# At a group's border, TensorE projects behind the contraction instead of in front of it, and VectorE takes first and adds later

## The reference, cut to what matters

```
x = x + conv(group_norm(x))      # 8 groups, 9 taps each, sampled bilinearly at learned places
    out = dcn_sample(v, deform, weights)      # v = x @ v_w + v_b
    return out.reshape(b, h, w, G * C) @ out_w + out_b
t = t + attention(layer_norm(t)) # 8 heads, 32 slices each: softmax(logits / temp), eidetic, out
t = t + experts(layer_norm(t))   # top 2 of 8 experts, 128 -> 512 -> gelu -> 128
```

## Time and profile before

| | us |
|---|---|
| median of 3 runs | 1312.51 |
| lowest and highest | 1308.49, 1313.44 |
| the profiled execution, its own time | 1311.18 |
| its span in the trace | 1309.4 |

### The profile page before, as it was taken

The page is one execution under the profiler, slowest core; times in us unless marked ns, Lnnn a source line. Parts: engine busy times, 40 slices in busy tenths (PEclk is TensorE's granted clock), DMA queues, the critical chain, the costliest instruction groups (busy, mean ns, idle before and its releaser), DMA issues.

```text
span 1309.4 us, 50781 instructions
## 1 busy us (share of the span) xinstructions
PE 992.3 (76%) x22310; PEld 807.6 (62%) x22310; DVE 829.8 (63%) x1651; ACT 773.7 (59%) x1431; POOL 688.0 (53%) x652
## 2 busy tenths in 40 slices
PE   4577785868788766998778758997887767787784
PEld 3455564656556655887466546886465656556684
DVE  5766757685766855557658746557578657446254
ACT  2676665777577572667767554667577545245352
POOL 2564545565645485444855693436755766003274
PEclk9689797998799787999988878999898878798997
DMA  6702130132100222364110322652110320444513
GB/s 161 158 24 53 54 68 23 68 56 68 28 26 19 58 80 76 113 176 119 48 48 24 97 72 70 172 167 63 48 41 25 108 82 3 133 132 142 162 43 95
DMA packets 142733, 104.80 MB, mean 80 GB/s; under 512 B 43649, under 2 KB 125890, under 8 KB 142002
## 3 DMA queue, kind: packets, MB, share of 16 engines
q1 hardware_dynamic: 138194, 92.68, 26.1%
q0 software_dynamic: 4320, 8.86, 2.3%
HBM read 76.32 MB, written 25.19 MB: 78 GB/s over the span
## 4 chain that ended last, share of the span: by engine, by line
PE 50%; ACT 17%; DVE 16%; issue 8%; POOL 7%; DMA 2%; SPq 0%; DVEq 0%; POOLq 0%; ACTq 0%
PE ps L1011 13%; PE ps L995 10%; PE ps L1226 6%; ACT xsb L1374 6%; PE ps L1019 5%; PE ps L1238 4%; DVE asb L1715 4%; ACT asb L1392 2%; POOL ysb L868 2%; PE ps L951 2%; POOL picked L834 2%; DVE ysb L1706 2%; DVE region L1942 2%; DVE x_tok L1985 2%; ACT region L1464 2%
## 5 line engine op out<-in xcount | busy, mean ns | idle before, releaser
L868 POOL TENSOR_TENSOR ysb<-ysb,rw 128x576 f32<-128x576 f32 x300 | 336.5, 1143 | 345.5 <-DVE ysb L1706 345.3
L995 PE MATMUL ps<-xsb,ysb 64*64 64x96 f32 x11008 | 328.6, 270 | 121.4 <-DVE asb L1715 30.1
L995 PEld LDWEIGHTS ps<-xsb,ysb 64*64 64x64 f32 x11008 | 278.3, 149 | 181.9 <-issue 89.0
L1374 ACT ACTIVATE xsb<-xsb,pick 128x576 f32<-128x576 f32 (+1 forms) x480 | 336.7, 751 | 5.2
L1715 DVE COPY asb<-ps 128x960 f32<-128x960 f32 (+1 forms) x208 | 215.9, 1044 | 115.9 <-PE ps L1011 106.0
L857 POOL TENSOR_TENSOR ysb<-rw,count 128x576 f32<-128x576 f32 (+1 forms) x150 | 174.8, 1165 | 70.6 <-PE ps L995 70.0
L1011 PE MATMUL ps<-asb,vd 32*32 32x258 f32 x8192 | 185.0, 391 | 24.4 <-issue 13.0
L1383 ACT ACTIVATE osp<-ps 128x258 f32<-128x258 f32 x128 | 43.0, 444 | 249.2 <-PE ps L1011 249.2
L1011 PEld LDWEIGHTS ps<-asb,vd 32*32 32x32 f32 x8192 | 124.6, 103 | 74.2 <-issue 42.4
L1464 ACT ACTIVATE region<-ps,b_col 128x128 f32<-128x128 f32 x368 | 104.9, 369 | 103.3 <-PE ps L1226 103.1
L1692 DVE TENSOR_TENSOR xsb<-rw,ps 128x576 f32<-128x576 f32 (+1 forms) x150 | 108.0, 720 | 54.7 <-PE ps L995 53.8
(11 more groups left out here) (304 smaller groups left out, 1203.3 us busy)
## 6 DMA issues: line engine op xcount, KB each, us to landing
ring<-in_L_ffn_W SPq DMA_DIRECT2D x122, 256.0 KB, 3.4
vd<-group_values SPq DMA_DIRECT2D x128, 128.0 KB, 2.7
set_rows<-ring SPq DMA_DIRECT2D x4, 1376.0 KB, 6.6
rw<-set_rows SPq DMA_DIRECT2D x30, 172.0 KB, 3.3
group_values<-region SPq DMA_DIRECT2D x32, 128.0 KB, 3.5
asb<-in_L_ffn_W SPq DMA_DIRECT2D x16, 256.0 KB, 5.1
region<-sorted_rows SPq DMA_DIRECT2D x6, 512.0 KB, 5.2
expert_rows<-region SPq DMA_DIRECT2D x6, 512.0 KB, 5.0
```

The costliest lines, as they stand in the source:

```text
L868: pl.tensor_tensor(ysb[:, ch % DEPTH, 0:sets, u, :], ysb[:, ch % DEPTH, 0:sets, NU - 1, :], rows_of(ig)[:, 2 + u, first:first + sets].rear ...
L995: last = pe.matmul(ps[64 * j:64 * j + 64, bank + i, NV * GRID * q:NV * GRID * (q + 1)], ysb[rows, ch % DEPTH, col, :, :].rearrange("p u y ...
L1374: act.activation(xsb[:, ch % DEPTH, 0:sets, v, :], xsb[:, ch % DEPTH, 0:sets, NV - 1, :], ACT.Relu, bias=pick[:, v:v + 1], scale=-1.0).the ...
```

## The change

Five things change together. At a border TensorE contracts first and projects behind that. On VectorE `conv_add` moves behind the border's `take`. TensorE's wait for `conv_add` stays at `at` = 1 where that slot has a side on TensorE (always in image 0) and goes to `at` = 2 elsewhere. Steps that stood in a slot just behind a border (11, 21, 71, 81) move one slot on: `temps` to 12, `turn_e0` to 22 (ScalarE's `exp1` to 20), and the tiles skip slots 71 and 81, so that the last is in slot 89. The picks and the adds follow by two slots (89 to 91, 101 to 103).

```
-PE_STEPS = {9: ("turn_tn",), 11: ("temps",), 16: ("logits0",), ...
-            21: ("turn_e0",), 23: ("turn_e1",), 25: ("sums",), ...
+PE_STEPS = {9: ("turn_tn",), 12: ("temps",), 16: ("logits0",), ...
+            22: ("turn_e0",), 23: ("turn_e1",), 25: ("sums",), ...
...
-             21: ("e0", "exp1"), 23: ("e1",), 25: ("sums",), 27: ("M",),
+             20: ("exp1",), 22: ("e0",), 23: ("e1",), 25: ("sums",), 27: ("M",),
...
-DVE_STEPS = {3: ("stats",), 6: ("normalise",), 8: ("bout",), 11: ("temps",), 12: ("recip0",), 14: ("recip1",),
+DVE_STEPS = {3: ("stats",), 6: ("normalise",), 8: ("bout",), 12: ("temps", "recip0"), 14: ("recip1",),
...
-TILE_SLOTS = tuple(range(64, 88))
-PICK_SLOT, PICK_SLOTS = 89, 12
-ADD_SLOT, ADD_SLOTS = 101, 5
+TILE_SLOTS = tuple(range(64, 71)) + tuple(range(72, 81)) + tuple(range(82, 90))
+PICK_SLOT, PICK_SLOTS = 91, 12
+ADD_SLOT, ADD_SLOTS = 103, 5
...
+            def has_side(b, slot):
+
+                return b == 0 or any(PE_STEPS.get(at) or turn_of(image_no, at) or tile_of(image_no, at)
+                                     for image_no, at in works(b, slot))
...
-                if at == 1 and ig >= 2:
+                if at == (1 if has_side(b, slot - slot % GROUP_SLOTS + 1) else 2) and ig >= 2:
                     pe.wait_ge(s.conv_added, ig - 1)
...
                 products(n)
                 if at == 0 and ig:
+                    contract(ig - 1)
                     if ig >= 2 and (ig - 1) % G:
                         wait_for_banks(b, slot + 1)
                         project(ig - 2)
-                    contract(ig - 1)
...
                 side(ig // G, n % SLOTS)
-                if at == 0 and ig >= 2 and (ig - 1) % G:
-                    conv_add(ig - 2)
-                elif at == 2 and ig and ig % G == 0:
+                if at == 2 and ig and ig % G == 0:
                     conv_add(ig - 1)
...
                 if not lifted(n):
                     take(n)
+                if at == 0 and ig >= 2 and (ig - 1) % G:
+                    conv_add(ig - 2)
```

More of the change, by code:

```diff
@@ L72 @@
 TURN_SLOT, JOIN_SLOT = 10, 12
-PE_STEPS = {9: ("turn_tn",), 11: ("temps",), 16: ("logits0",), 17: ("logits1",), 18: ("logits2",), 19: ("logits3",),
-            21: ("turn_e0",), 23: ("turn_e1",), 25: ("sums",), 26: ("eid",), 27: ("M",), 28: ("out",),
+PE_STEPS = {9: ("turn_tn",), 12: ("temps",), 16: ("logits0",), 17: ("logits1",), 18: ("logits2",), 19: ("logits3",),
+            22: ("turn_e0",), 23: ("turn_e1",), 25: ("sums",), 26: ("eid",), 27: ("M",), 28: ("out",),
             35: ("turn_xt",), 36: ("router",),
@@ L85 @@
              44: ("columns0",), 45: ("b2",), 46: ("columns1",), 47: ("columns2",)}
-ACT_LAST = {**ACT_STEPS, 20: ("exp1",), 19: ("logits3", "exp0"), 21: ("e0",)}
+ACT_LAST = ACT_STEPS
 DVE_LAST = {**DVE_STEPS, 38: (), 41: ("normalise2",)}
```

## The result

The changed kernel took 1349.2 us (median of 4 runs, 1341.4 to 1354.3) against 1313.0 before: 1.026 times the time, 95% interval 1.022 to 1.030. The forecast was 1344 us, range 1312 to 1354. The profiled execution took 1354.3 us, span 1352.5; that is 5 above its median, so a sum made from the two traces (43.1 us) is larger than the difference of the medians (36).

What follows compares the result with a forecast made beforehand. The prediction saw a chain that changes engines all the time, TensorE busiest with half of it, ScalarE, VectorE and GpSimd 41%. Its terms summed to +32.9 us on the profiled 1311.2, forecasting 1344 us, range 1312 to 1354.

Steps and rivals of the forecast that it cites:

- E: Slot 20 of images 2 and 3: late picks hold VectorE's adds, so `bdE` starts 23 us behind the contraction; +12.5 us.
- C: Slot 10 of images 1 to 3: `temps` in slot 12 delays VectorE's chain to the first logits by 1.65 each; +5.0 us.
- the first kind: 20 of 27 borders, where the previous slots are copied before TensorE finishes; the contraction starts 2.0 us earlier.
- B: Slot 0 of image 1: the projection of image 0's last group, in slot 2, waits for the add too; +1.6 us.
- D: Slot 20 of image 1: the projection adds 1.1 us, an earlier `exp1` gives a little back; +1.0 us.
- I: Slot 60 of images 1 to 3: TensorE waits for the add before the turned rows in slot 61; +4.2 us.
- G: Slot 40 of images 1 to 3: products start later, slot 42 waits for the add, delaying the sort; +4.8 us.
- J: Tiles, images 0 to 3: empty slots 71 and 81, and a last tile two slots later pushing `turn_tn`; +2.4 us.
- A: Image 0: three queries in slots 21, 41, 61 come 1.3 us later each, other borders cancel; +4.0 us.
- F: Slot 30 of images 1 to 3: the contraction starts 0.65 earlier until the last copy binds; -1.5 us.
- the rival of 1354 us: All adds before `bdE` run beside GpSimd, with C's upper end: 1354 us; chance 0.09 shared with another rival.
- The rival on the other side: Faster, because the path leaves the contraction through ScalarE at the borders: -12 us, 1299 us; chance 0.1.

Runs made afterwards that it cites:

- e3: The changed kernel with the slots of tiles, picks and adds put back as before: 1345.2 us, 1.028 times the kernel before.
- e5: The changed kernel with only the picks and adds back in their slots (89 and 101): 1347.7 us, 1.026 times the kernel before.

## Why the prediction was right, and where its sizes were off

**Right by its own steps.** The two kinds of borders, the wait for the add as the new price, and the late picks with their chain to `bdE` show in the trace as they were written (as a sum E is 10.5 us, not the largest: C has 12.0). At the first kind the contraction now follows the border's products at once (0.07 us before their end at 12 of the 20), and the products behind come 1.91 us after it, the projection's length. Where a side with L951 or L1210 stands between, they come 4.3 to 4.5 us after it: the 3.3 of the forecast and the side. Terms B, D, E, H, I and K are within 2 us of the forecast, and the kernels with one half of the change, with the late slots back and with the adds away show whose E, G and I are.

**Too small: C, G and J, 18 us together.** C's own step, the moved temperatures, cost 3.9 instead of 5.0; what the sum left out is the granted clock, 11 us in images 1 and 2. The extra matmuls show that it hangs on the idle time ahead; the traces with the old steps show that it falls without the change as well, so most of this error is the luck of two traces. For G the step was right (projection and add between contraction and products), but the sum let the contraction keep its length. The products of slot 41 end 2.1 to 2.8 us later: 0.9 to 1.0 of that is the projection, as allowed, and 1.1 to 1.3 the slower contraction, 3.6 us over the three images (in image 2 it also starts 0.8 later). With the 4.8 of the forecast this makes 8.4 of the 10.0; what the rest is, is not shown. For J the mechanism is the one named, the last tile in slot 89 pushes `turn_tn` behind VectorE's copies: slots 0 to 10 get 5.5 and 4.0 shorter with the tiles back in their slots (e3), but not with the picks and adds alone back (+7.6 and +8.2, e5). It costs 6.3 and 6.6 there, of which about 2.1 is the tile that came over from slots 70 to 80. That J is as large with the swap alone, the prediction did not have: its J prices the moved tiles.

**Too large: A and F.** A's three queries paid the 1.3 us each, as the wait list shows, and their stretches lost 6.2 us in all; but the stretches of the three other swapped borders gained 4.0 where I had them cancel, and slots 0 to 20 gained 1.1. F gained 6.1 instead of 1.5; the moved tables alone have 2.9 of it without any swap, and what brings that is open.

**The sum.** (In E, 23 less 17.6 and 15.6 is 5.4 and 7.4, so the forecast's own figures give 12.8 and not 12.5.) The large errors, 2.8 + 4.6 + 2.0 us too much in A, F and E against 7.0 + 5.2 + 6.0 too little in C, G and J, came out with the small ones at 10 us too little on the profiled execution and 5 on the median. That the median fell so near the forecast is partly luck of this kind. The rule of the Trainium skill, "SBUF — State Buffer", section "Who interferes with whom", did no more to the changed kernel than forecast: three trios of adds at the faster of their two speeds and one at the slower, not all at the slower, as the rival of 1354 us had it. In the kernel with the adds away it does decide: a step of 0.16 us took 4.19 beside GpSimd.

**The rival on the other side.** It fails: the swap alone is 2.8% slower. Why the earlier contraction gained so little is in part its clock: at the 20 borders of the first kind the contractions take 133.2 us instead of 118.0. Whether the path left the contraction through ScalarE at too few places as well, no run here tests.

## What to carry to other kernels

A job that moves from in front of a long step to behind it takes its follower along: here the add lost the contraction as its cover, and the busier engine waited for it at most borders. The job can also have been filling a wait of its own engine: without the projection ahead of it, the contraction ran at a lower clock. Look for what stands in the queue ahead of a chain's next step (16 adds that nobody needs yet, ahead of `bdE`), and put it where its engine waits for another anyway; that alone gave 0.9%. A place with idle time is not enough: if another engine waits for the very next instruction there, as for the tiles' copies, the time is only moved.

## What the runs showed of the hardware

Short idle times of TensorE ahead of a busy stretch can be dearer than themselves: 2.9 us of waiting stood ahead of 20.7 us at half clock, of work that takes 14.8 at full. They need not be: behind the same 2.9 us the work took 14.9 us in two other traces. Filled with matmuls, they cost nothing of the kind in six of six places. TensorE was busy for 20.56 of the 20.70 us, so a stretch without a gap can run nearly to its end at the lower level. And the same slots of one kernel differ by this: in the changed kernel 20.7, 20.7 and 17.3, in the kernel with the old steps 17.3, 23.05 and 15.2, before 15.1, 14.8 and 17.3. Executions of one kernel spread by 1% (the changed kernel's four: 1354.3, 1352.6, 1345.8 and 1341.4 at mean clocks of 0.864, 0.866, 0.868 and 0.883), so single stretches have to be compared over several kernels before a term can be told from the clock.

A tiny step of VectorE that reads two tiles took 0.16 us in the changed kernel and 4.19 beside GpSimd's elementwise instructions, for as long as these followed one another without a gap.
